# Two graph layers in fp32 on one core: x turned by DVE and moves, masked exponentials in place, new instruction orders

## The chip, the cores and the metric

The kernel runs on one core of a Trainium2 chip. The metric is the device time of one execution in microseconds (us). The core has a matrix engine (TensorE, PE in the profile, with its weight loads as PEld), three engines for elementwise work (VectorE, DVE; ScalarE, ACT; GpSimd, POOL), and an engine that here does nothing but start transfers (SyncE, SP). Each engine runs its own instructions in the order in which they are written, and waits on semaphores for the others.

## What is computed

Eight batches, each with 1024 nodes of 128 channels and a 1024 x 1024 adjacency matrix of zeros and ones, all in fp32. Two layers with a norm each:

```python
u = x @ x.T / sqrt(128)                      # 1024 x 1024 per batch
delta = softmax(u) * adj
att = delta / (sum(delta, axis=2) + 1e-10)
# left: j > i, self: j == i, right: j < i; h_k = x @ W_k.T + b_k
ctx = att_left @ h_left + att_self @ h_self + att_right @ h_right
x1 = norm(x + relu(ln_w * norm(ctx) + ln_b))
d = (sum(adj, axis=-1) + 1e-5) ** -0.5
out = norm(x1 + (d_i * adj * d_j) @ (x1 @ W1) + b1)
```

## The kernel before

A batch is cut into eight blocks i of 128 rows, and into two halves of four blocks (HB = 4). For each block, PE makes the scores u (`scores`, six matmuls of 512 columns, since x is split into a high and a low part in a faster format), DVE takes the row maximum (`row_max`), ACT the exponential (`exps`), DVE multiplies it by the adjacency rows and sums (`masked`), PE turns the product by eight transposes (`turn_d`), ACT copies it out of the accumulator memory (`d_out`), and PE multiplies it with the projected rows (`context_far`, and `context_near` for the diagonal block, for which POOL makes three masked copies in `masks`). Each `project` of a block is followed by `add_bias` on DVE, for the projections share one bank, ps_m.

The second layer needs the adjacency matrix turned. DVE turns it in squares of 32 x 32 (`turn_blocks`, from a_rows to a_blk), and sixteen on-chip transfers for each half (`move_blocks`, issued by SP, L280) put the squares where they belong: in aT, for the last batch in a_rows itself. `gather` multiplies them with the rows of the first layer (x1p), `second_product` with W1 into ps_m, and `add_out` and `stats_f` on DVE follow it. The norms c, x and f each go through DVE (`stats_*`), POOL (`scale_*`), and ACT or POOL.

x itself is also needed turned. Before, PE does that in every batch: `turn_x(b, k)` makes four transposes (L397) for half k into ps_m; ACT's `x_high` (L775) copies them, scaled and rounded, to xT_hi, and DVE's `x_low` (L1027) subtracts to get xT_lo. The exponentials go to e_rows, the masked ones to d_rows, two buffers each: `exps(g)` waits for `masked(g-2)`, and `masked(g)` for `turn_d(g-2)`.

The order of the work on each engine is written out by hand in three functions, `first_batches` (batches 0 and 1), `batch` (2 to 6, in a loop) and `last_batches` (7, the last); b is the batch whose scores are made, p the one before, whose second layer runs beside it. In `batch` PE opens with `turn_x(b, 0)`, `scores(p, 7)`, `turn_d(p, 5)`, `turn_x(b, 1)`. SP takes loads, moves and stores in one order too: a wait on one holds up all behind it.

Of the kernel before, what the change touches and what calls it, by code (L numbers as in the profile page):

```python
# [11 lines left out]
P = 128  # L12
Q = 32
# [12 lines left out]
def two_layer_graph_kernel(nc, x, adj, Wl, bl, Ws, bs, Wr, br, ln_w, ln_b, W1, b1, out):  # L26
# [5 lines left out]
    MOVES = 16 * NQ * NQ  # L32
    SHRINK = float(H) ** -0.25
    assert H == P and NB == 8 and HALF == 512

    with ExitStack() as ctx:  # L36
# [11 lines left out]
        wraw = sb("wraw", [P, 3, H])  # L48
# [10 lines left out]
        xT_lo = sb("xT_lo", [P, 2, N], F32R)  # L59
        h_sum = sb("h_sum", [P, 2, NB, 3 * H])  # L60
# [3 lines left out]
        e_rows = sb("e_rows", [P, 2, N])  # L64
        d_rows = sb("d_rows", [P, 2, N])
# [6 lines left out]
        fin = sb("fin", [P, NB, H])  # L72
        junk = sb("junk", [P, N], mybir.dt.bfloat16)
# [37 lines left out]
        xt_tr = sem("xt_tr")  # L111
        xt_hi = sem("xt_hi")
# [83 lines left out]
        def x_bank(b, k):  # L196
            return ps_y[:, :] if b == 0 and k else ps_m[:, :]
# [54 lines left out]
        def _(sp):  # L252
            def load_x(b):
                wait(sp, xt_tr, 2 * (b - 1))
                wait(sp, x_added, NB * (b - 1))
                sp.dma_start(x_rows[:, b % 2, :, :], x_block_rows(x, b, 0, N)).then_inc(x_in[b % 2], 16)
# [26 lines left out]

            def load_weights():
# [15 lines left out]
            def first_batches(b, p):  # L300
# [5 lines left out]
                next_x(p)  # L306
                load_a(p, 1)
                load_norm_constants()
                load_a(p, 2)
                load_a(p, 3)  # L310
                load_a(p, 4)
                load_a(p, 5)
                next_a(p, 0)
                load_a(p, 6)
                load_a(p, 7)
                next_a(p, 1)
# [4 lines left out]
                next_a(p, 5)  # L321
                move_blocks(p, 1)
                next_a(p, 6)
                next_a(p, 7)
                next_x(b)
                next_a(b, 0)
                store(p, 0, HB)
                next_a(b, 1)
                next_a(b, 2)
                next_a(b, 3)  # L330
                move_blocks(b, 0)
                store(p, HB, NB)
                next_a(b, 4)
                move_blocks(b, 1)
                next_a(b, 5)
                next_a(b, 6)
                next_a(b, 7)

            def batch(b, p):

# [3 lines left out]
                next_a(b, 2)  # L344
                next_a(b, 3)
                store(p, 0, HB)
                move_blocks(b, 0)
                next_a(b, 4)
                store(p, HB, NB)
                next_a(b, 5)  # L350
                next_a(b, 6)
                move_blocks(b, 1)
                next_a(b, 7)

            def last_batches(b, p):

                move_blocks(b, 0)
# [1229 lines left out]
```

## Time and profile before

| | us |
|---|---|
| median of 3 runs (463.78 to 465.43) | 463.79 |
| the profiled execution, its own time | 465.88 |
| its span, first to last instruction | 464.2 |
| PE busy | 449.6 |
| DVE busy | 385.9 |
| ACT busy | 296.0 |
| POOL busy | 296.0 |

The page gives the busy time of each engine over the span; the windows give it for a stretch, the waits say who stood idle for whom, and the timelines list instructions by their start. A row of PE that is merged from several matmuls lasts a little longer than the engine needs for them, since they are pipelined: the distance of two starts is what counts. The granted clock of PE is 0.993 over the span.

### The profile page before, as it was taken

Reading aid. Unit: us, or ns where it says so; the run is one execution under the profiler, and the core shown is the slowest. Engines: PE = TensorE matmul, PEld = TensorE weight load, DVE = VectorE, ACT = ScalarE, POOL = GpSimd, SP = SyncE. Lnnn points to the kernel's source line nnn. Section 1 sums busy time; section 2 is a strip of 40 time slices with the busy share of each in tenths; the row PEclk is TensorE's granted clock in tenths of the full one; section 3 lists DMA queues with packets and bytes.
Section 4 is the critical chain, followed back from the end, with each engine's and each line's share of the span. In section 5 each row is a group of like instructions: output and inputs, shape, how many; then the busy total and the mean of one; then the engine's idle time right before and its main releaser. Section 6 shows DMA issues by size and latency. Waiting matters only on the chain. (4 is left out here: it accounts for less than half of the span.)

```text
span 464.2 us, 8778 instructions
## 1 busy us (share of the span) xinstructions
PE 449.6 (97%) x2711; PEld 364.3 (78%) x2711; DVE 385.9 (83%) x678; ACT 296.0 (64%) x611; POOL 296.0 (64%) x364
## 2 busy tenths in 40 slices
PE   7999999999999999999999999999999999999793
PEld 4799987697967978599776997769886798877562
DVE  3989998898878898788888988789897887998705
ACT  2867787785574876566685765658558676757410
POOL 2324766678655867468663875739665578678762
PEclk9999999999999999999999999999999999999988
DMA  7654739695860897418981289804997066377701
GB/s 174 244 179 114 209 80 241 189 237 141 250 227 1 197 272 208 142 45 195 271 236 73 72 200 270 277 1 108 256 222 234 0 165 200 72 188 172 183 23 45
DMA packets 64269, 76.72 MB, mean 165 GB/s; under 512 B 5696, under 2 KB 56000, under 8 KB 64224
## 3 DMA queue, kind: packets, MB, share of 16 engines
q1 hardware_dynamic: 64160, 76.11, 61.2%
q8 instruction: 22, 0.36, 0.4%
q14 instruction: 23, 0.19, 0.1%
q0 software_dynamic: 64, 0.07, 0.1%
HBM read 38.40 MB, written 4.19 MB: 92 GB/s over the span
## 5 line engine op out<-in xcount | busy, mean ns | idle before, releaser
L783 ACT ACTIVATE e_rows<-ps_u,nmax 128x1024 f32<-128x1024 f32 x62 | 69.0, 1113 | 69.9 <-DVE nmax L1036 69.6
L449 PE MATMUL ps_c<-h_sum,dT 128*128 128x128 f32 x896 | 110.4, 275 | 0.0
L1373 POOL TENSOR_TENSOR dM<-dT,parts 128x384 f32<-128x384 f32 x64 | 68.4, 1068 | 64.9 <-ACT dT L790 55.8
L449 PEld LDWEIGHTS ps_c<-h_sum,dT 128*128 128x128 f32 x896 | 107.0, 192 | 2.5 <-issue 1.4
L469 PE MATMUL ps_y<-aT,x1p 128*128 128x512 f32 x224 | 101.7, 592 | 0.0
L1036 DVE TENSOR_REDUCE nmax<-ps_u 128x1 f32<-128x1024 f32 x62 | 75.5, 1217 | 22.7 <-PE ps_u L376 22.2
L1044 DVE CUSTOM_DVE_ANT_0 d_rows<-e_rows,a_rows 128x1024 f32<-128x1024 f32 x64 | 84.9, 1327 | 7.8 <-PE ps_d L434 7.7
L790 ACT ACTIVATE dT<-ps_d 128x1024 f32<-128x1024 f32 x64 | 65.2, 1018 | 27.7 <-PE ps_d L434 21.3
L1051 DVE STREAM_TRANSPOSE a_blk<-a_rows 128x1024 f32<-128x1024 f32 x64 | 77.9, 1230 | 0.0
L469 PEld LDWEIGHTS ps_y<-aT,x1p 128*128 128x128 f32 x224 | 40.8, 190 | 37.8 <-issue 37.3
L434 PE MATMUL ps_d<-parts,d_rows 128*128 128x128 f32 x512 | 66.8, 273 | 1.4 <-DVE dsum L1044 1.2
L796 ACT ACTIVATE junk<-a_rows 128x1024 bf16<-128x1024 f32 x64 | 67.1, 1048 | 0.7 <-DMA a_rows<-in_adj_dram 0.5
L434 PEld LDWEIGHTS ps_d<-parts,d_rows 128*128 128x128 f32 x512 | 58.3, 141 | 9.7 <-DVE dsum L1044 3.9
L374 PE MATMUL ps_u<-xT_hi 128*128 128x512 f32 x124 | 56.3, 454 | 0.0
L376 PE MATMUL ps_u<-xT_hi,xT_lo 128*128 128x512 f32 x124 | 49.0, 395 | 0.0
L375 PE MATMUL ps_u<-xT_lo,xT_hi 128*128 128x512 f32 x124 | 48.8, 394 | 0.0
L247 DVE TENSOR_TENSOR h_sum<-ps_m,bias_bc 128x384 f32<-128x384 f32 x64 | 35.3, 552 | 8.5 <-PE ps_m L376 6.3
L455 PE MATMUL ps_c<-h_sum,dM 128*128 128x128 f32 x256 | 39.0, 275 | 0.0
L1438 POOL TENSOR_TENSOR power_f<-var_f,minus_half 128x4 f32<-128x4 f32 (+1 forms) x17 | 16.6, 977 | 32.1 <-DVE nmean_f L1130 32.1
L455 PEld LDWEIGHTS ps_c<-h_sum,dM 128*128 128x128 f32 x256 | 34.3, 192 | 1.4 <-issue 1.4
L231 POOL TENSOR_TENSOR c_rows<-c_rows,lnw_bc 128x512 f32<-128x512 f32 x15 | 25.1, 1674 | 13.9 <-ACT c_rows L809 13.9
L1413 POOL TENSOR_TENSOR power_x<-var_x,minus_half 128x4 f32<-128x4 f32 (+1 forms) x17 | 22.5, 1324 | 17.7 <-DVE var_x L1107 17.6
(92 smaller groups left out, 710.7 us busy)
## 6 DMA issues: line engine op xcount, KB each, us to landing
a_rows<-in_adj_dram SPq DMA_DIRECT2D x64, 512.0 KB, 5.2
aT<-a_blk SPq DMA_DIRECT2D x224, 128.0 KB, 2.4
x_rows<-in_x_dram SPq DMA_DIRECT2D x8, 512.0 KB, 5.1
a_rows<-a_blk SPq DMA_DIRECT2D x32, 128.0 KB, 2.4
out_dram<-fin SPq DMA_DIRECT2D x15, 256.0 KB, 2.7
out_dram<-fin SPq DMA_DIRECT2D x2, 128.0 KB, 1.8
wraw<-in_L_gnn_Wl_dram SPq DMA_DIRECT2D x1, 64.0 KB, 3.4
wraw<-in_L_gnn_Wr_dram SPq DMA_DIRECT2D x1, 64.0 KB, 3.1
```

Of the source, the lines that this page charges most:

```text
L374: pe.matmul(o, hi_l, hi_r, start=True, stop=False)
L434: last = pe.transpose(ps_d[:, j, :], d_rows[:, i % 2, j * P:(j + 1) * P], ident)
L449: pe.matmul(ps_c[:, c_place(b, i), :], dT[:, i % 2, j, :], h_sum[:, b % 2, j, k * H:(k + 1) * H], start=t == 0, stop=False)
L455: last = pe.matmul(ps_c[:, c_place(b, i), :], dM[:, i % 2, k, :], h_sum[:, b % 2, i, k * H:(k + 1) * H], start=False, stop=k == 1)
L469: last = pe.matmul(y_bank(b, i0, i1), gathered(b)[:, j, :], turned(b)[:, i0:i1, :, j, :].rearrange("p i q c -> p (i q) c"), start=j == 0, ...
L783: act.activation(e_rows[:, i % 2, :], u_bank(b, i), ACT.Exp, bias=nmax[:, i % 2:i % 2 + 1], accum_out=zsum[:, i:i + 1]).then_inc(exp_done, 1)
L790: act.activation(dT[:, i % 2, :, :], ps_d[:, :, :], ACT.Copy).then_inc(dt_out, 1)
L796: act.activation(junk[:, :], a_rows[:, i, :], ACT.Copy, accum_out=deg[:, i:i + 1])\
L1036: dve.tensor_reduce(nmax[:, i % 2:i % 2 + 1], u_bank(b, i), AX.X, ALU.max, negate=True)\
L1044: dve.tensor_tensor_reduce(out=d_rows[:, i % 2, :], in0=e_rows[:, i % 2, :], in1=a_rows[:, i, :], scale=1.0, scalar=0.0, op0=ALU.mult, op1 ...
L1051: dve.transpose(a_blk[:, i, :, :, :], a_rows[:, i, :].rearrange("p (j m c) -> p m j c", m=NQ, c=Q))\
L1373: pool.tensor_tensor(dM[:, i % 2, :, :], dT[:, i % 2, i, :].rearrange("p (a c) -> p a c", a=1).to_broadcast([P, 3, P]), parts[:, :, :], AL ...
```

## The change

- From batch 2 on, `turn_x` on PE is gone. `turn_rows(b)` on DVE turns the rows of batch b+1 in squares of 32 x 32, `move_rows(b)` on SP puts them into x_turned by sixteen transfers, and `x_high` and `x_low` read from there; `x_low` takes two instructions of 256 elements for each half in place of one of 512 and has both inputs in SBUF.
- The exponentials are written to d_rows, a ring of three, and masked there in place. `exps(g)` now waits for `turn_d(g-3)`, and `masked` no longer waits for PE. e_rows is gone.
- wraw lies in fin. Two of the four first matmuls are shortened from 512 to 384 columns.
- All engines have new orders. `scores(b, 7)`, `turn_d(b, 5)`, `turn_d(b, 6)`, `context_far(b, 4)` and `(b, 5)` and `context_near(b, 4)` are now in batch b's own part; the moves of half 1 go to the start of the next part on SP. In `first_batches` DVE turns the first adjacency block ahead of the first row maximum. In `last_batches` PE makes the last contexts ahead of most of the previous batch's gathers of half 1.

```diff
@@ helpers
+        def x_columns(b, k):
+            if b < 2:
+                return (ps_y if b == 0 and k else ps_m)[:, :]
+            return x_turned[:, NQ // 2 * k:NQ // 2 * (k + 1), :, :]
...
+        def x_pieces(v, b):
+            return [v] if b < 2 else [v[:, q, :, :] for q in range(NQ // 2)]
@@ sync
+            def move_rows(b):
+                sp.wait_ge(rows_turned, b)
+                if b > 1:
+                    sp.wait_ge(xt_split, 2 * (b + 1))
+                for q in range(NQ):
+                    for m in range(NQ):
+                        sp.dma_start(x_turned[m * Q:(m + 1) * Q, q, :, :], x_blk[q * Q:(q + 1) * Q, m, :, :])\
+                          .then_inc(rows_moved, 16)
...
+            def batch(b, p):
+
+                move_blocks(p, 1)
+                next_a(p, 7)
+                next_x(b)
+                next_a(b, 0)
+                next_a(b, 1)
+                move_rows(b)
+                next_a(b, 2)
+                move_blocks(b, 0)
                 next_a(b, 3)
                 store(p, 0, HB)
-                move_blocks(b, 0)
                 next_a(b, 4)
+                next_a(b, 5)
                 store(p, HB, NB)
-                next_a(b, 5)
                 next_a(b, 6)
-                move_blocks(b, 1)
-                next_a(b, 7)
@@ tensor, batch: its start and its end
+                scores(b, 0)
+                m_read_o(p - 1, HB, NB)
+                project(b, 0)
+                context_near(p, 5)
+                turn_d(p, 7)
...
                 second_product(p, HB, NB)
-                context_far(b, 3)
-                context_near(b, 3)
+                context_far(b, 4)
+                turn_d(b, 6)
+                context_near(b, 4)
+                context_far(b, 5)
@@ tensor, last_batches: from the last scores to the first gather of half 1
                 scores(b, 7)
+                context_far(b, 4)
                 m_read_h(b, 7)
                 second_product(p, 0, HB)
+                context_near(b, 4)
+                turn_d(b, 6)
                 gather(p, HB, NB, 0, 1)
                 context_far(b, 5)
                 gather(p, HB, NB, 1, 2)
+                turn_d(b, 7)
                 context_near(b, 5)
                 context_far(b, 6)
                 context_near(b, 6)
                 context_far(b, 7)
                 context_near(b, 7)
+                gather(p, HB, NB, 2, 4)
+                gather(p, HB, NB, 4, 6)
+                gather(p, HB, NB, 6, 8)
+                m_read_o(p, 0, HB)
+                second_product(p, HB, NB)
+                gather(b, 0, HB, 0, 4)
+                gather(b, HB, NB - 2, 0, 2)
@@ scalar
             def exps(b, i):
                 g = NB * b + i
                 act.wait_ge(nmax_ready, g + 1)
-                wait(act, d_ready, g - 1)
+                wait(act, dt_tr, g - 2)
@@ vector
-                wait(dve, dt_tr, g - 1)
-                dve.tensor_tensor_reduce(out=d_rows[:, i % 2, :], in0=e_rows[:, i % 2, :],
+                dve.tensor_tensor_reduce(out=d_rows[:, g % 3, :], in0=d_rows[:, g % 3, :],
...
+            def turn_rows(b):
+                dve.wait_ge(x_in[(b + 1) % 2], 16 * ((b + 1) // 2 + 1))
+                wait(dve, rows_moved, ROW_MOVES * (b - 1))
+                dve.transpose(x_blk[:, :, :, :],
+                              x_rows[:, (b + 1) % 2, :, :].rearrange("p i (m c) -> p m i c", m=NQ, c=Q))\
+                   .then_inc(rows_turned, 1)
@@ vector, first_batches
                 add_bias(p, 0)
+                turn_blocks(p, 0)
                 row_max(p, 0)
@@ vector, batch: its start, the place of turn_rows, its end
+                x_low(b, 0)
+                x_low(b, 1)
+                masked(p, 7)
+                turn_blocks(p, 7)
...
+                stats_x(p, HB, NB)
+                turn_blocks(b, 1)
                 masked(b, 3)
+                turn_blocks(b, 2)
+                row_max(b, 5)
                 row_sums(b, 0)
                 turn_blocks(b, 3)
+                turn_rows(b)
                 masked(b, 4)
...
+                row_max(b, 7)
+                add_self(b, 0, HB)
+                stats_c(b, 0, HB)
                 masked(b, 6)
                 add_out(p, HB, NB)
                 stats_f(p, HB, NB)
@@ vector, last_batches: between the last row maximum and the last turned block
+                row_max(b, 7)
+                add_out(p, 0, HB)
+                stats_f(p, 0, HB)
+                masked(b, 7)
                 turn_blocks(b, 4)
                 turn_blocks(b, 5)
+                stats_x(b, 0, HB)
                 turn_blocks(b, 6)
                 turn_blocks(b, 7)
```

## Rows read from the trace of the kernel before

**Rows 1.** The page: busy us, share of the span, instructions of each engine.

```profile
PE 449.6 (97%) x2711; PEld 364.3 (78%) x2711; DVE 385.9 (83%) x678; ACT 296.0 (64%) x611; POOL 296.0 (64%) x364
```

**Rows 2.** Windows: one batch; busy us (instructions) by engine, PEclk, DMA share, GB/s.

```profile
172.08:227.66 55.58, 55.15 (x337) 44.79 (x337) 47.94 (x83) 36.54 (x78) 36.59 (x44) 1.00 0.63 169
```

**Rows 3.** Waits of PE, 5 to 440 us: waiter, releaser, total us, times, longest.

```profile
PE ps_d L434 <- DVE dsum L1044: 1.2, 3, 0.4
```

**Rows 4.** Timeline, start of the last batch: start us, us, engine, line, operation, count.

```profile
371.10 0.60 PE L397 MATMUL ps_m<-parts,x_rows 128*128 128x128 f32 x4
371.54 1.04 PE L434 MATMUL ps_d<-parts,d_rows 128*128 128x128 f32 x8
```

**Rows 5.** Two lines of DVE by tile and line: duration ns min/median/max, first and last start.

```profile
L1027 DVE SCALAR_TENSOR_TENSOR xT_lo<-ps_m,xT_hi x15: 653/686/692, 6.8 to 372.4; 128x512 fp32r<-128x512 f32 x15
...
L1102 DVE SCALAR_TENSOR_TENSOR c_rows<-c_rows,x_rows x17: 426/1418/1486, 52.0 to 440.4; 128x512 f32<-128x512 f32 x15, 128x256 f32<-128x256 f32 x2
```

**Rows 6.** Timeline of POOL and DVE in one stretch.

```profile
225.52 0.99 POOL L1373 TENSOR_TENSOR dM<-dT,parts 128x384 f32<-128x384 f32 x1
225.67 1.92 DVE L1044 CUSTOM_DVE_ANT_0 d_rows<-e_rows,a_rows 128x1024 f32<-128x1024 f32 x1
...
227.99 1.21 DVE L1044 CUSTOM_DVE_ANT_0 d_rows<-e_rows,a_rows 128x1024 f32<-128x1024 f32 x1
```

**Rows 7.** Lines L280 and L256 (SP): durations ns, and issue to landing.

```profile
L280 SPq DMA_DIRECT2D aT<-a_blk x224: 591/606/1902, 41.3 to 410.5; - x112
...
DMA to landing us min/median/max: 2.3/2.4/6.8
...
DMA to landing us min/median/max: 3.8/5.1/8.5
```

**Rows 8.** Timeline of SP: one group of sixteen moves.

```profile
261.93 12.41 SPq L280 DMA_DIRECT2D aT<-a_blk  x16
```

**Rows 9.** The start: PE, DVE, and the landing of the first adjacency block.

```profile
13.33 0.41 PE L374 MATMUL ps_u<-xT_hi 128*128 128x512 f32 x1
...
10.67 1.21 DVE L1036 TENSOR_REDUCE nmax<-ps_u 128x1 f32<-128x1024 f32 x1
...
L263 SPq DMA_DIRECT2D a_rows<-in_adj_dram x1: 432/432/432, 4.3 to 4.3; - x1
...
DMA to landing us min/median/max: 7.3/7.3/7.3
```

**Rows 10.** Timeline of PE from the last scores to the last batch's gathers.

```profile
417.04 1.05 PE L481 MATMUL ps_m<-w_sb,yT 128*128 128x128 f32 x8
...
419.49 1.02 PE L469 MATMUL ps_y<-aT,x1p 128*128 128x512 f32 x2
420.35 0.61 PE L455 MATMUL ps_c<-h_sum,dM 128*128 128x128 f32 x4
420.80 1.73 PE L449 MATMUL ps_c<-h_sum,dT 128*128 128x128 f32 x14
422.36 1.04 PE L434 MATMUL ps_d<-parts,d_rows 128*128 128x128 f32 x8
...
440.54 3.95 PE L469 MATMUL ps_u<-a_rows,h_sum 128*128 128x256 f32 x10 [2.85 <-DMA a_rows<-a_blk]
```

**Rows 11.** What precedes the last moves: DVE, ACT, and SP (410 to 442 us).

```profile
423.81 2.36 DVE L1051 STREAM_TRANSPOSE a_blk<-a_rows 128x1024 f32<-128x1024 f32 x2
...
425.58 1.06 ACT L796 ACTIVATE junk<-a_rows 128x1024 bf16<-128x1024 f32 x1
...
L280 SPq DMA_DIRECT2D a_rows<-a_blk x32: 585/602/2141, 414.7 to 438.0; - x32
```

**Rows 12.** Windows: the stretch after PE's last long wait, columns as in rows 2.

```profile
440.00:444.00 4.00, 3.46 (x9) 2.83 (x10) 1.41 (x5) 1.59 (x4) 2.95 (x6) 0.57 0.23 66
```

**Rows 13.** Timeline of DVE: add_out and the end of stats_f.

```profile
452.88 1.13 DVE L1118 SCALAR_TENSOR_TENSOR fin<-ps_m,dinv,x1b 128x128 f32<-128x128 f32 x4 [11.18 <-PE ps_m L481]
...
454.99 0.16 DVE L1130 TENSOR_SCALAR nmean_f<-stats_f 128x4 f32<-128x4 f32 x1
```

More of the change, by code:

```diff
@@ L305, in first_batches @@
                 load_a(p, 0)
-                next_x(p)
                 load_a(p, 1)
@@ new lines, in first_batches @@
+                turn_d(p, 7)
+                m_read_h(b, 2)
+                project(b, 3)
+                scores(b, 2)
+                context_near(p, 6)
+                m_read_h(b, 3)
+                project(b, 4)
+                context_far(p, 7)
+                m_read_h(b, 4)
+                project(b, 5)
+                context_near(p, 7)
+                scores(b, 3)
+                turn_d(b, 0)
+                gather(p, 0, HB, 0, 1)
+                m_read_h(b, 5)
+                project(b, 6)
@@ new lines, in first_batches @@
+                gather(p, 0, HB, 1, 3)
+                scores(b, 4)
+                m_read_h(b, 6)
+                project(b, 7)
+                gather(p, 0, HB, 3, 4)
+                turn_d(b, 1)
+                context_far(b, 0)
+                context_near(b, 0)
+                context_far(b, 1)
+                turn_d(b, 2)
+                scores(b, 5)
+                context_near(b, 1)
+                turn_d(b, 3)
+                context_far(b, 2)
+                turn_d(b, 4)
@@ new lines, in first_batches @@
+                context_near(b, 2)
+                context_far(b, 3)
+                gather(p, 0, HB, 4, 8)
+                scores(b, 6)
+                gather(p, HB, NB, 0, 1)
+                context_near(b, 3)
+                gather(p, HB, NB, 1, 2)
+                m_read_h(b, 7)
+                second_product(p, 0, HB)
+                gather(p, HB, NB, 2, 4)
+                gather(p, HB, NB, 4, 7)
+                scores(b, 7)
+                gather(p, HB, NB, 7, 8)
+                turn_d(b, 5)
@@ new lines, in first_batches, with batch @@
+                m_read_o(p, 0, HB)
[4 more added lines that the diff above has]
+                turn_d(b, 6)
+            def batch(b, p):
+                scores(b, 0)
+                m_read_o(p - 1, HB, NB)
+                project(b, 0)
+                context_near(p, 5)
+                turn_d(p, 7)
+                m_read_h(b, 0)
+                project(b, 1)
+                context_far(p, 6)
```

827 lines of the change are left out of this document (371 added, 456 removed).

## The prediction

> **What bounds the kernel now.** I read the page first, then windows of one batch, then the waits of the engine they point to. PE is busy for 449.6 of 464.2 us, DVE for 83% of it [rows 1]. The share alone could mislead, for a merged row of PE covers its pipeline's latency too, so the window of one batch decides: PE busy for 55.15 of 55.58 us, at a granted clock of 1.00, which is 2.4 GHz [rows 2]. The waits say the same from the other side: between 5 and 440 us the costliest wait of PE, turn_d for the masked rows, comes to 1.2 us in three places [rows 3]. So between the start and the end the time is the sum of PE's own work, and an edit gains what it takes off PE, unless it makes PE wait. Outside that stretch there are two losses: the start (PE waits for the first data and biases) and the end, where PE stands idle 2.85 us for the last on-chip moves [rows 10] and then runs at a granted clock of 0.57 in the mean of 4 us [rows 12], between the two levels of 2.4 and 1.2 GHz: (1 - 0.57) x 4 = 1.7 us more.
>
> **The change part by part, in PE's time.**
>
> Removed: turn_x of batches 2 to 7, twelve times four transposes. What four cost is the distance of two starts, 371.54 - 371.10 = 0.44 us [rows 4] (the 0.60 us of the row itself has the pipeline's latency in it). 12 x 0.44 = 5.3 us. This is certain as work, since no other instruction of PE takes its place, and it is the whole gain that the trace supports directly. The two shortened first matmuls run before the first data can be used; I cost that at nothing, for the first add_bias waits for the bias loads anyway.
>
> Added on DVE: turn_rows, six transposes of 128 x 1024. Two of the kind take 2.36 us [rows 11], so 1.2 each, 7 us in all. x_low: before, two instructions of 0.686 us a batch [rows 5]. After, four of 256 elements, both inputs in SBUF. The nearest row is stats_x's addition in L1102, whose 256-wide form is the minimum of 426 ns [rows 5]; back to back they overlap a little, so 1.5 to 1.7 us. The other bound is the same line's 512-wide form in its usual state, 1418 ns: four half-wide ones then come to 2 x 1.42 = 2.84 us. DVE rises from 385.9 to about 395 us, which it has room for; what matters is where. x_low stands at the border of two batches, and scores(b, 0) is now the first thing that PE wants of the new one. After the previous second_product PE has left: context_far(4), turn_d(6), context_near(4), context_far(5). By distances of starts a context_far is 422.36 - 420.80 = 1.56, a context_near 420.80 - 420.35 = 0.45 [rows 10], a turn_d eight transposes, 0.88 [rows 4]: 4.45 us. In that time DVE must do add_out and stats_f, which take 454.99 + 0.16 - 452.88 = 2.27 us [rows 13], and x_low, 1.5 to 1.7: 3.8 to 4.0, and some 0.2 for hand-overs. That just fits; I take 0 to 0.3 us of PE idle a border, six borders.
>
> What may stretch x_low is in the trace. masked took 1.92 us while POOL's masks ran beside it and 1.21 without [rows 6]; L1102, which has the same kind of inputs, is nearly always in the long state. x_low from PSUM never is: 653 to 692 ns over all its uses [rows 5]. The Trainium skill (GPSIMD Engine Reference, 1. Specifications) says that POOL contends for SBUF with DVE instructions that have two SBUF inputs. By that rule the new x_low is exposed and the old was not, which speaks against this part; the trace agrees on masked and on L1102. By order of the lists POOL has scale_f and then affine near the border, and affine waits for ACT's norm_c, which stands behind x_high; so I take the short state and keep the long one as a rival.
>
> Added on SP: sixteen moves a batch. An aT move of 128 KB takes 0.606 us to issue [rows 7], and a group of sixteen 12.4 us [rows 8]; these are a quarter of the size, so at most that. SP then has three groups a batch, at most 37 us, and some ten loads and stores, in a batch of 55: it fits. The chain in time, counted from scores(b, 0): stats_x(p, HB) lets go of the x rows at about 25 us, the load lands 5.1 us later (8.5 at worst) [rows 7], at 30 to 33; turn_rows stands behind seven DVE steps and is done at about 34; the moves are out at 46 and landed at 48 to 49 (2.4 us [rows 7]); x_high wants them at about 50. Margin 1 to 2 us, more if the smaller moves issue faster. Queued behind the group are next_a(b, 2) and move_blocks(b, 0); the first needs no more than to land before the next batch's third masked, the second is wanted only at the next batch's first gather, some 14 us into it. Both come in time.
>
> In place and in a ring of three: same instruction, same size. L1102 writes over its own input too, and its 256-wide 426 ns [rows 5] are in line with masked's 1.21 us for 1024 elements out of place [rows 6], so in place costs nothing that a row shows. exps(g) now waits for turn_d(g-3), which in the new orders is always three steps earlier, and masked loses its wait for PE. Price 0 on both, and the cover is PE's saturation.
>
> The orders, in the middle: with all steps at their rows' durations, the hand-over that is nearest to late is exps(3) before scores(4), within 0.2 us. Now PE idles 55.58 - 55.15 = 0.43 us a batch; I expect 0.3, for a gain of 0.8 us over six or seven batches. Bounds: -2.5 (all idle gone) to +4.
>
> The start: turn_blocks(p, 0) now stands ahead of row_max(p, 0), which began at 10.67; it needs the adjacency block that was issued at 4.3 and landed 7.3 us later, at 11.6, and takes 1.2: row_max begins at 12.8, 2.1 us later. exps(0) is as much later, and PE's scores(2), which began at 13.33 [rows 9], waits for it. Some of it is had back, since idle times that stood behind it are filled: +1.0 us, bounds 0 and +2.1.
>
> The end, counted from the end of scores(7), 417.04 [rows 10]. Before: DVE is done turning at 423.81 + 2.36 = 426.17, ACT with the degrees at 426.64, the last of the moves starts at 438.0 [rows 11], PE goes on at 440.54, 13.5 us after the start of the sixteen moves at about 427.0. After, DVE does: row_max 1.2, wait for second_product (PE: context_far 1.56, eight matmuls 0.9) until 2.6, add_out and stats_f 2.3, masked 1.3, two turns 2.4, stats_x 2.1, two turns 2.4: 13.1. With 13.5 for the moves: 26.6. PE gets there after four context_far (6.2), four context_near (1.8), two turn_d (1.8), two second_product (1.8), and gathers of eight steps at 420.35 - 419.49 = 0.86 (6.9) and of the first four of the last batch (3.4): 21.9. So the wait is 4.7 us, not 2.85, and the slow clock behind it stays at 1.7. One of the two waits for yT at the very end is filled by a gather, -0.7. Sum of the end: +1.9 - 0.7, rounded down to +0.9, since a wait of ACT or POOL may as well shrink. This is the second unsure term: bounds -5 (moves in time, clock kept) and +3.
>
> Sum: -5.3 - 0.8 + 1.0 + 0.9 = -4.2 us on the profiled 465.88, whose span is 464.2; the same difference on the median of the runs, which lies 2.1 below the profiled execution: 463.79 - 4.2 = 459.6.
>
> **The rivals.**
> A, x_low in the long state, or DVE late at the border. The long x_low is 1.2 us more than the short one, of which 0.2 is margin: 1.0 a border, six borders: 459.6 + 6 = 465.6; if every second one is hit, 462.6. For it: the long state of L1102. Against: what stands on POOL there. The trace of after shows it as PE idle before scores(b, 0).
> B, slower: SP. The rows of x come late since SP is one queue: the x load waits for stats_x(p, HB, NB), and the moves behind it for turn_rows. The x load at its worst landing (3.4 us later than the median) and moves at the full cadence put x_high 2 to 4 us behind, and PE has nothing before scores(b, 0) that could run: each us over the margin costs one at six borders. It outweighs the gain from 0.7 us a border on; with 2 us it gives 459.6 + 12 = 471.6.
> C, the last moves are in time. PE's wait and the slow clock are gone: 459.6 - 4.7 - 1.7 = 453.2. For it: PE has 2 us more work ahead of the wait than before. Against: DVE turns the last blocks some 4 us later.
> That the change doesn't do what it says is no rival: the transposes are gone by the text.
>
> **How the numbers follow.** My case 0.64 (its own range 456.5 to 461.5), A 0.18, B 0.08, C 0.10. The range reaches down into C and up into A: 455 to 465. A measurement of this kernel can tell 0.5%, 2.3 us, from no change: faster is below 461.5, slower above 466.1. Faster: 0.62 of my case, 0.10 of C, 0.03 of A: 0.75. Slower: 0.08 of B and 0.02 of A: 0.10. Same: 0.15.
>
> **What would show it.** L397 on PE sixteen times, in place of 64, and the windows' PE work lower by 0.88 us a batch; PE's busy share in a batch of the middle still above 99%, the batch 54.6 to 54.9 us long. x_low's instructions at 0.43 us (my case) or 0.7 (A). PE's wait for xT_lo or xT_hi at the borders under 0.3 us (else A or B; B if x_high waits for the moves). The last wait for the moves at 4 to 5 us (else C). Wrong would be above all a PE that waits in the middle of batches for nmax, exponentials or h_sum, which I costed at 0.3 us a batch.

## The result and the profile after

The changed kernel takes 463.38 us in the median of 20 runs (461.15 to 465.00), the kernel before 464.73 us of 20 (463.49 to 466.19). The ratio of the means is 0.9964, 95% interval 0.9951 to 0.9977: 1.7 us less (1.35 by the medians), where 4.2 us less was forecast. It is faster, then, but by less than the 0.5% that the forecast took as the least to tell from no change, and it lies 1.9 us above the 461.5 below which it would have been called faster. The range of 455 to 465 us holds the time. In the runs further below, one execution, of the kernel with all edits and two queues, took 925.38 us, about twice the others, and is left out of every median, ratio and product.

The page's row for PE (busy us, share of the span, instructions), which answers to [rows 1]; the span of this execution is 461.6 us, its time 463.36 us:

```profile
PE 444.2 (96%) x2663; PEld 357.7 (77%) x2663; DVE 388.8 (84%) x696; ACT 296.8 (64%) x611; POOL 310.9 (67%) x364
```

PE lost 5.4 us of busy time and 48 instructions, yet the span fell by 2.6 us only: PE's idle time rose from 464.2 - 449.6 = 14.6 to 461.6 - 444.2 = 17.4 us. To find where, I cut both executions into the same three stretches (columns as in [rows 2]). Before:

```profile
0.00:60.00 60.00, 56.76 (x362) 49.32 (x363) 48.83 (x76) 38.68 (x76) 23.73 (x33) 1.00 0.61 178
60.00:360.00 300.00, 298.91 (x1805) 241.04 (x1804) 260.06 (x444) 202.68 (x422) 200.61 (x236) 1.00 0.67 180
360.00:464.20 104.20, 93.92 (x548) 73.95 (x546) 76.98 (x161) 54.65 (x114) 71.61 (x96) 0.97 0.47 117
```

After, and below it one batch of the middle, from scores(b, 0) to the next scores(b, 0):

```profile
0.00:60.00 60.00, 53.34 (x338) 45.20 (x339) 46.90 (x70) 39.09 (x77) 23.66 (x34) 1.00 0.61 195
60.00:360.00 300.00, 299.67 (x1800) 241.14 (x1799) 267.98 (x468) 203.81 (x422) 213.31 (x238) 1.00 0.67 182
360.00:461.60 101.60, 91.23 (x529) 71.41 (x527) 73.90 (x160) 53.88 (x115) 73.90 (x94) 0.97 0.52 133
...
176.34:230.64 54.30, 54.23 (x329) 43.91 (x329) 48.10 (x86) 36.84 (x77) 39.46 (x45) 1.00 0.69 184
```

Idle is the length less PE's busy time. In the first 60 us it went from 3.24 to 6.66: 3.4 us more, at a granted clock of 1.00 in both. In the middle it went from 1.09 to 0.33, 0.8 less, and at the end from 10.28 to 10.37. So the middle gave what was forecast, the end cost 0.1, and the start idled 3.4 more where I had written 1.0. The batch of 54.30 us stands against the 55.58 of [rows 2].

Not all of the 3.4 is lost time. These are the first matmuls and the first projection, before and then after:

```profile
1.51 3.78 PE L392 MATMUL ps_u<-d_rows 128*128 128x512 f32 x4 [1.51 <-DVE d_rows L1016]
...
8.12 0.41 PE L374 MATMUL ps_m<-wT_hi,xT_hi 128*128 128x384 f32 x1 [0.85 <-DVE wT_lo L1020]
...
1.51 3.35 PE L421 MATMUL ps_u<-d_rows 128*128 128x512 f32 x4 [1.51 <-DVE d_rows L1038]
...
7.52 0.41 PE L403 MATMUL ps_m<-wT_hi,xT_hi 128*128 128x384 f32 x1 [1.26 <-DVE wT_lo L1042]
```

The shortened first matmuls give PE 0.4 us less to do and the wait for the low weights is 0.4 longer, yet the first projection starts 0.6 us sooner. So 0.4 us only passed from busy to idle: some 3.0 us are lost in the start, and 5.0 of the 5.4 us of busy time are other work.

The waits of PE between 5 and 440 us show the same (waiter, releaser, total us, times, longest); in [rows 3] the costliest of before was 1.2:

```profile
PE ps_m L403 <- DVE h_sum L263: 3.7, 4, 1.4
PE ps_m L403 <- DVE wT_lo L1042: 1.3, 1, 1.3
PE ps_c L478 <- issue: 0.9, 1, 0.9
PE ps_m L510 <- issue: 0.8, 1, 0.8
```

All four waits for h_sum (add_bias, L263) lie before 52 us: 0.88 at 10.60, 1.40 at 14.18, 0.80 at 23.88 and 0.65 at 51.20 us; the same line took 0.5 in all before. The first is no loss: before, PE went on at 10.81 there, and the two other profiled executions of the changed kernel have three such waits, 2.9 in sum. The other three, 2.85 us, are nearly the whole 3.0. The timeline of DVE for the one at 14.18 (start us, us, line, tiles), with PE's row below it:

```profile
11.31 1.25 DVE L1074 STREAM_TRANSPOSE a_blk<-a_rows 128x1024 f32<-128x1024 f32 x1 [0.77 <-DMA a_rows<-in_adj_dram]
12.47 1.19 DVE L1060 TENSOR_REDUCE nmax<-ps_u 128x1 f32<-128x1024 f32 x1
13.58 0.54 DVE L263 TENSOR_TENSOR h_sum<-ps_m,bias_bc 128x384 f32<-128x384 f32 x1
...
14.18 0.44 PE L403 MATMUL ps_m<-wT_hi,xT_hi 128*128 128x384 f32 x1 [1.40 <-DVE h_sum L263]
```

turn_blocks(p, 0) waits 0.77 us for the adjacency block and takes 1.25. The row maximum stands behind it, and behind that the bias of step 1, without which project(2) has no PSUM to write to. So the moved transpose is paid by PE not through the exponentials, as I had reasoned, but through add_bias.

The waits at 23.88 and 51.20 have another origin. There PE's new list has two projections with nothing between them (the earlier ones start at 22.31 and 49.86; in the old list a scores, a turn_d or a context stands between), and the second must wait until add_bias, 0.55 us, has emptied ps_m. DVE's row and PE's at the later place:

```profile
50.58 0.56 DVE L263 TENSOR_TENSOR h_sum<-ps_m,bias_bc 128x384 f32<-128x384 f32 x1 [0.21 <-PE ps_m L405]
...
51.20 0.45 PE L403 MATMUL ps_m<-wT_hi,xT_hi 128*128 128x384 f32 x1 [0.65 <-DVE h_sum L263]
```

DVE had itself stood idle 0.21 us for PE, so nothing in DVE's list was in the way. At 23.88 masked was, until 23.28, for about 0.3 us of that wait.

**One quantity used below.** Executions of one and the same kernel differ by 2 to 4 us, and nearly all of it is the mean granted clock: the 20 of the changed kernel stand in groups near 0.989, 0.993 and 0.996, and span times clock has a standard deviation of only 0.4 us around 458.4 (457.5 to 459.3). I call that product the span at full clock. It is 461.0 and 460.7 for the kernel before in two sets, and 458.7 and 458.8 for the changed one beside it. It strips the clock from a comparison; the runs' ratio keeps it, and is the time that counts. With few executions its scatter is 0.4 to 1.0 us, so differences of 0.7 are near what it can tell.

The profiled executions show where the groups come from. In two of the changed kernel's three, the stretches from 440 to 448 us have a lowered clock (0.71 and 0.86 in one, 0.63 and 0.94 in another); the third, with the same wait of 2.2 us before them, has none:

```profile
440.00:444.00 4.00, 3.11 (x11) 2.20 (x12) 1.63 (x8) 1.76 (x4) 2.89 (x8) 1.00 0.16 46
444.00:448.00 4.00, 3.65 (x16) 2.07 (x15) 0.00 (x0) 0.60 (x1) 3.62 (x8) 1.00 0.03 8
```

Their means are 0.993, 0.993 and 0.996. Other executions lose about as much in the first 60 us (0.66 from 8 to 12 us in the run with the turned block later, mean 0.992), and one with a lowered clock near both ends (0.57 from 8 to 12 us and 0.83 from 430 to 440, in the kernel with all edits and two queues) has 0.989. Such a stretch is worth about 1.7 us, (0.29 + 0.14) x 4 in the first, and whether it comes differs between executions of one kernel.

### The profile page after: what moved, and what is told of

It reads as the page before. It is cut to its first block and busy times, and to the rows that moved or that the text cites. A ratio compares the mean times of both kernels' runs of the same rounds, so it can differ in the third digit from the quotient of the medians.

```text
span 461.6 us, 8799 instructions
## 1 busy us (share of the span) xinstructions
PE 444.2 (96%) x2663; PEld 357.7 (77%) x2663; DVE 388.8 (84%) x696; ACT 296.8 (64%) x611; POOL 310.9 (67%) x364
## 5 line engine op out<-in xcount | busy, mean ns | idle before, releaser
L498 PE MATMUL ps_y<-aT,x1p 128*128 128x512 f32 x224 | 104.3, 592 | 0.0
L805 ACT ACTIVATE d_rows<-ps_u,nmax 128x1024 f32<-128x1024 f32 x62 | 68.9, 1112 | 50.3 <-DVE nmax L1060 50.2
L1067 DVE CUSTOM_DVE_ANT_0 d_rows<-d_rows,a_rows 128x1024 f32<-128x1024 f32 x64 | 84.8, 1326 | 0.4 <-ACT d_rows L805 0.4
L498 PEld LDWEIGHTS ps_y<-aT,x1p 128*128 128x128 f32 x224 | 39.7, 190 | 29.9 <-issue 29.4
L263 DVE TENSOR_TENSOR h_sum<-ps_m,bias_bc 128x384 f32<-128x384 f32 x64 | 35.3, 551 | 14.7 <-PE ps_m L405 12.4
L484 PEld LDWEIGHTS ps_c<-h_sum,dM 128*128 128x128 f32 x256 | 36.0, 191 | 4.5 <-issue 2.9
L255 POOL TENSOR_SCALAR fin<-fin,power_f,shift_f 128x128 f32<-128x128 f32 x56 | 36.2, 659 | 0.3
L1421 POOL TENSOR_TENSOR power_c<-var_c,minus_half 128x4 f32<-128x4 f32 (+1 forms) x17 | 22.2, 1304 | 20.1 <-DVE nmean_c L1119 20.1
L403 PE MATMUL ps_m<-wT_hi,xT_hi 128*128 128x384 f32 x64 | 28.4, 444 | 5.0 <-DVE h_sum L263 3.7
```

The lines of the kernel that those rows point to most:

```text
L403: pe.matmul(o, hi_l, hi_r, start=True, stop=False)
L484: last = pe.matmul(ps_c[:, c_place(b, i), :], dM[:, i % 2, k, :], h_sum[:, b % 2, i, k * H:(k + 1) * H], start=False, stop=k == 1)
L498: last = pe.matmul(y_bank(b, i0, i1), gathered(b)[:, j, :], turned(b)[:, i0:i1, :, j, :].rearrange("p i q c -> p (i q) c"), start=j == 0, ...
L805: act.activation(d_rows[:, g % 3, :], u_bank(b, i), ACT.Exp, bias=nmax[:, i % 2:i % 2 + 1], accum_out=zsum[:, i:i + 1]).then_inc(exp_done, 1)
L1067: dve.tensor_tensor_reduce(out=d_rows[:, g % 3, :], in0=d_rows[:, g % 3, :], in1=a_rows[:, i, :], scale=1.0, scalar=0.0, op0=ALU.mult, op1 ...
```

## The experiments

The theory: PE's sum is the time; the removed transposes came off it whole, and what is missing went into waits of PE at the start, by the orders of DVE's and PE's lists, with small ones at the end. Rivals: the work removed isn't worth its pitch, the new path of x costs something in the middle, or the missing time is the wait for the last moves. Each kernel below is an edit of the changed one, and ratios are to the kernel before. The changed kernel itself ran as a mark in two of the sets.

**The changed kernel again.**

> The changed kernel once more, on the chip of the runs beside it, as their mark. Theory: 1.3 to 2.5 us faster than the kernel before; the mean granted clock of its executions is about 0.0015 lower than that of the kernel before (0.7 us of a span), because it has more idle time of PE at the start and at the end, behind which the clock is granted late. Rival (the clock is the chip's, not the kernel's): the mean clocks agree within 0.0005.

Measured 462.95 us, ratio 0.9954 (0.9931 to 0.9977). The mean clocks are 0.9944 for the kernel before and 0.9939 for this one, the 0.0005 of the rival and not the 0.0015 of the theory.

> The changed kernel once more, beside the others of this set: 0.995 to 0.998 of the kernel before, span times clock 458.4 to 458.8.

Measured 462.55 us, ratio 0.9960 (0.9943 to 0.9977). Full-clock spans as above.

**Is PE the sum?** 48 transposes that nothing reads, written to ps_y behind the second product of six batches:

```
+    def idle_turns():
+        for j in range(8):
+            pe.transpose(ps_y[:, j % 4 * P:(j % 4 + 1) * P], ident, ident)
...
     second_product(p, HB, NB)
+    idle_turns()
```

> The changed kernel with eight more transposes on PE in each of batches 1 to 6, after the second product of half 1, that turn the identity into a free bank and that nobody reads: 48, as many as the change took away. Theory (PE is the sum): the gain of the transposes is given back in full, 5.3 us slower than the changed kernel, ratio to the kernel before 1.007 to 1.009, each batch of the middle 0.88 us longer than 54.3. Rival (PE has slack in the changed kernel, and DVE or the exponentials set its pace): under 2 us slower.

Measured 470.35 us, ratio 1.0106 (1.0076 to 1.0137); full-clock span 464.4, which is 5.7 to 6.0 above the changed kernel. The work added is 48 x 0.11 = 5.3 us by the pitch of [rows 4]. In time it is 6.9 us above the changed kernel, more than the 1.007 to 1.009 expected, since its mean clock is 0.9915. The middle of its profiled execution is as full as that of the changed kernel, so nothing absorbed it:

```profile
60.00:360.00 300.00, 299.67 (x1821) 242.87 (x1821) 262.56 (x458) 200.31 (x414) 210.67 (x233) 1.00 0.67 182
```

So 48 transposes are worth their pitch in either direction, and the term of -5.3 us stands. The few tenths above it are, in part, a last wait for the moves that is longer by 0.7 us in that execution; that part isn't settled.

**The turned block ahead of the first row maximum.**

```
     add_bias(p, 0)
-    turn_blocks(p, 0)
     row_max(p, 0)
...
     add_bias(p, 7)
+    turn_blocks(p, 0)
     turn_blocks(p, 1)
     row_max(p, 5)
```

SP also asks for batch 1's first adjacency block two loads later; that was not tried apart.

> The changed kernel, but at the start DVE turns the first adjacency block only just ahead of the second one, and SP asks for batch 1's first block two loads later; all else is as changed. Theory (start): the changed kernel loses its gain in the first 60 us, where PE idles 3.4 us more than in the kernel before, 1.8 us of that since the first row maximum starts at 12.47 instead of 10.67 us. Then this run is 1.5 to 2 us faster than the changed kernel, ratio to the kernel before 0.992 to 0.993, and the idle time before the third projection (1.4 us) goes. Rival (idle time moves on): the first exponentials then meet other waits, and the run is within 0.5 us of the changed kernel, ratio 0.996.

Measured 460.96 us, ratio 0.9908 (0.9886 to 0.9930), full-clock span 457.2 in four executions: 1.2 to 1.5 us under the changed kernel of the other sets (458.4 to 458.7), a little less than expected. The wait at 14.18 is gone, one of 0.7 for the exponentials came, the two behind it (23.88 and 51.20) stayed. So this line costs what the term of +1.0 had been written for, and the rest of the 3.0 stays.

**The whole old start.** First only the lists up to the fifth row maximum; DVE's edit, with PE's, ACT's and SP's lists taken back likewise:

```
     add_bias(p, 0)
-    turn_blocks(p, 0)
     row_max(p, 0)
     add_bias(p, 1)
     row_max(p, 1)
-    masked(p, 0)
-    row_max(p, 2)
     add_bias(p, 2)
-    row_max(p, 3)
+    masked(p, 0)
     add_bias(p, 3)
-    masked(p, 1)
+    row_max(p, 2)
...
+    row_max(p, 4)
+    masked(p, 3)
+    turn_blocks(p, 0)
     turn_blocks(p, 1)
```

> The changed kernel with the old order of scores, projections, row maxima and masked steps up to the fifth row maximum, on PE, DVE, ACT and SP. Theory (start): the whole loss of the first 30 us comes back, 2.5 to 3 us against the changed kernel, ratio to the kernel before 0.989 to 0.991; turn_x of batch 1 starts some 2.7 us earlier than in the changed kernel. Rival (only the turned block matters): the same as the run with the block turned later, within 0.4 us. Second rival: the time is given back before 60 us, where add_bias and the row maxima are late.

Measured 463.53 us, ratio 0.9960 (0.9939 to 0.9981), full-clock span 458.1. My graft made a wait of its own: scores(5) stood at once behind turn_d(2) and waited 2.0 us for the exponentials. So this run said little of the 2.5 to 3 us expected, and I grafted the order up to scores(6), with DVE's and ACT's steps beside it (PE's edit, against the first graft):

```
     turn_d(p, 2)
-    scores(p, 5)
     m_read_h(p, 7)
     turn_x(b, 0)
     context_far(p, 0)
     context_near(p, 0)
+    scores(p, 5)
     context_far(p, 1)
```

> As the run with the old start, but with the old order carried on to the sixth scores: these stand behind turn_x of batch 1 and the first contexts again, so that PE has work while ACT makes the fifth exponentials. Theory (the loss is in the order of the start, and the 2.2 us wait at 26 us of the run before was made by the graft): PE's idle time in the first 60 us falls from 9.2 to 6 or 7 us, 2.3 to 3 us faster than the changed kernel in the same call. Rival (the idle time moves on to the steps that follow, whose order expects the new start): within 1 us of the changed kernel.

Measured 461.88 us, ratio 0.9911 (0.9888 to 0.9935), full-clock span 457.0. The window and the waits from 5 to 60 us:

```profile
0.00:60.00 60.00, 54.76 (x346) 47.20 (x347) 48.34 (x72) 40.77 (x79) 26.11 (x35) 1.00 0.65 197
...
PE ps_m L403 <- DVE wT_lo L1042: 1.3, 1, 1.3
PE ps_u L403 <- ACT d_rows L805: 1.1, 1, 1.1
PE ps_m L403 <- DVE h_sum L263: 1.0, 2, 0.7
```

PE is busy 1.42 us more than in the changed kernel, which agrees with 1.7 less at full clock. The h_sum waits fell from 3.7 to 1.0. The gain expected, 2.3 to 3, is missed. PE's busy time is still 2.0 short of before: 0.4 is the shortened first matmuls and no loss, 1.1 is a wait for exponentials that the graft places late, and 0.5 is more h_sum, since 0.65 at 49.6 us remains in the second batch, whose order I left alone.

**The new path of x with the old orders.** The moves of x go into SP's old list ahead of move_blocks(b, 0), turn_rows behind turn_blocks(b, 3), and the lists of PE, DVE and ACT stay those of before but for what the path itself adds and removes. On SP, against the changed kernel:

```
-    move_blocks(p, 1)
-    next_a(p, 7)
-    next_x(b)
     next_a(b, 0)
+    next_x(b)
     next_a(b, 1)
-    move_rows(b)
     next_a(b, 2)
-    move_blocks(b, 0)
     next_a(b, 3)
+    move_rows(b)
     store(p, 0, HB)
+    move_blocks(b, 0)
...
     next_a(b, 6)
+    move_blocks(b, 1)
+    next_a(b, 7)
```

> The changed kernel's x path and ring of three, but all lists of steps as in the kernel before, less turn_x from batch 2 on and with turn_rows and move_rows put in after the turn of block 3. Theory (PE is the sum, the orders are not what gains): 4.5 to 5.5 us faster than the kernel before, ratio 0.988 to 0.990, faster than the changed kernel, since the start is the old one. Rival (the new orders are needed, for with the old ones PE waits at the border for x_low or for row maxima): 0 to 2.5 us faster than before, with waits of PE of 0.5 to 1 us a batch.

Measured 470.35 us, ratio 1.0110 (1.0089 to 1.0131), full-clock span 462.4. DVE, SP, ACT and PE at the border of the second and third batch:

```profile
85.60 1.25 DVE L1085 STREAM_TRANSPOSE x_blk<-x_rows 128x1024 f32<-128x1024 f32 x1 [0.29 <-DMA x_rows<-in_x_dram]
...
88.83 1.73 SPq L280 DMA_DIRECT2D a_rows<-in_adj_dram  x3
90.62 10.08 SPq L308 DMA_DIRECT2D x_turned<-x_blk  x16
100.81 11.17 SPq L297 DMA_DIRECT2D aT<-a_blk  x16
...
102.02 0.63 ACT L801 ACTIVATE xT_hi<-x_turned 128x512 fp32r<-128x512 f32 x1 [9.74 <-DMA x_turned<-x_blk]
...
103.70 1.09 PE L463 MATMUL ps_d<-parts,d_rows 128*128 128x128 f32 x4 [7.79 <-ACT dT L816]
```

The x rows are turned at 86.85, but SP, behind three loads in its list, starts the sixteen moves at 90.62 and needs 10.08 us for them. ACT stands still 9.7 us for the first, with d_out queued behind it, and PE 7.8 us. That is rival B's mechanism, once. At four later borders PE waits 0.23 to 0.24 us for x_low, and a batch takes 54.8 us. The run is 5.1 us slower than the kernel before, outside both the theory (4.5 to 5.5 faster) and its rival (0 to 2.5 faster). At full clock it is 1.3 slower; the rest is clock, 0.987 in the mean against 0.995, with 0.66 from 104 to 108 us, behind the wait. So the new orders are no ornament of the change: they pull the moves of x out of the way and bring 0.5 us a batch (54.3). Other places for the moves in the old list weren't tried.

**The end: the added bias ahead of masked.** PE's idle 0.92 us at 396.99 (context_far(0), which reads h_sum) has these rows of POOL and DVE in front of it:

```profile
393.23 2.09 POOL L1464 TENSOR_TENSOR x1b<-x1b,b_bc 128x512 f32<-128x512 f32 x1
...
392.14 2.02 DVE L1067 CUSTOM_DVE_ANT_0 d_rows<-d_rows,a_rows 128x1024 f32<-128x1024 f32 x1
...
394.10 2.31 DVE L1067 CUSTOM_DVE_ANT_0 d_rows<-d_rows,a_rows 128x1024 f32<-128x1024 f32 x1
...
396.34 0.55 DVE L263 TENSOR_TENSOR h_sum<-ps_m,bias_bc 128x384 f32<-128x384 f32 x1
```

Two masked take 2.02 and 2.31 us beside POOL's additions of 128 x 512, and 1.2 at the start without them. The edit:

```
     masked(b, 2)
-    masked(b, 3)
     add_bias(b, 7)
+    masked(b, 3)
```

> One edit on the changed kernel: in the last batch the added bias of step 7 stands ahead of masked of step 3. Theory (the 1.06 us that PE idles at 397 before the first far product is the wait for that bias behind a stretched masked): the wait is gone or under 0.3 us, masked of step 3 and what hangs on it come some 0.8 us later without PE waiting for it, span times clock lower by 0.8 to 1.1 us. Rival (the time comes back as a longer wait for the last moves, which stand behind DVE's list): wait at 440 longer by as much, sum unchanged.

Measured 462.16 us, ratio 0.9955 (0.9932 to 0.9978); full-clock span 457.5, 1.25 below the mark of its set. PE doesn't wait there any more, and DVE's second masked, now behind the bias, starts 0.5 us later against the first and takes 1.83. The runs' ratio, though, is that of the mark, since its executions had a mean clock of 0.993 where the mark had 0.995. Its wait for the last moves is 2.1 us, as before the edit, so the rival (it comes back there) falls; in time, the 1 us can't be told from nothing by these runs.

**The end: the last two turned blocks first.**

```
     turn_blocks(b, 5)
-    stats_x(b, 0, HB)
     turn_blocks(b, 6)
     turn_blocks(b, 7)
+    stats_x(b, 0, HB)
```

> One edit on the changed kernel: the last two turned blocks stand ahead of the sum of x (2.1 us) in the last batch. Theory (the last wait for the moves is the time by which DVE hands over the last turned block): the sixteen moves start some 2 us earlier and the wait of 2.3 us before the last gathers goes to under 0.5 us; the half of the output that needs the sum of x comes 2 us later and the wait of PE for it, 0.9 us, grows by up to 2 us, so the sum is 0 to 1.5 us lower. Rival (PE's order gives it all back): no change in span times clock.

Measured 461.18 us, ratio 0.9928 (0.9903 to 0.9952), full-clock span 458.1, 0.7 below the mark, which its scatter (456.6 to 458.8 in six executions) doesn't tell from nothing. PE's wait for the moves (2.2 us in the changed kernel) is gone from the list, and 0.7 for the sum of x came:

```profile
PE ps_m L510 <- issue: 1.1, 2, 0.8
...
PE ps_y L498 <- ACT h_sum L831: 0.7, 1, 0.7
```

In time it brings 1.4 us, twice what it brings at full clock: its six executions have a mean clock of 0.997 (0.995 to 0.998), the mark's twelve 0.995 (0.992 to 0.997).

**The end: half of the last moves on ACT.**

```
+    def move_rest(b):
+        act.wait_ge(a_turned, NB * (b + 1))
...
+        for q in range(NQ // 2, NQ):
+            for m in range(NQ):
+                act.dma_start(turned(b)[m * Q:(m + 1) * Q, blocks_of(1), q, :, :],
+                              a_blk[q * Q:(q + 1) * Q, blocks_of(1), m, :, :])\
+                   .then_inc(a_moved[1], 16)
...
     diagonal(b, 7)
+    move_rest(b)
     norm_x(b, 0, HB)
```

SP keeps the eight with q below NQ // 2.

> The changed kernel, but of the last sixteen moves (last batch, half 1) ACT issues eight, between diagonal(7) and norm_x. Theory (SP's issue of 0.65 us a move sets the end of PE's wait at 440.6): the moves are all out 5 us earlier, the wait of 2.4 us and the slow clock behind it (1.7 us in the profiled run) go, 2.4 to 4 us faster than the changed kernel, if norm_x stays in time on ACT. Rival (something else arrives no earlier: the rows of the first layer, at 441 to 443 us): the wait is replaced by one for x1p, under 1 us faster.

Measured 464.15 us, ratio 0.9971 (0.9955 to 0.9988), full-clock span 459.4, 0.7 above the mark, where 2.4 to 4 faster was expected. The timeline of ACT and PE:

```profile
428.47 6.30 ACTq L841 DMA_DIRECT2D a_rows<-a_blk  x8
434.88 1.65 ACT L831 ACTIVATE h_sum<-c_rows,shift_x,scale_x 128x128 f32<-128x128 f32 x4 [6.96 <-issue]
436.43 0.57 ACT L860 ACTIVATE yT<-ps_y 128x512 f32<-128x512 f32 x1
...
437.10 2.04 PE L510 MATMUL ps_m<-w_sb,yT 128*128 128x128 f32 x8 [3.36 <-issue]
```

The wait for the moves is gone, but ACT spends 6.30 us on issuing eight of them, y_out stands behind, and PE waits 3.36 us for yT, where it had waited 0.78. A queue on an engine that does other work isn't a free queue.

**Together.** The edits above in one kernel: the old start (the second graft), the bias ahead of masked, the two turned blocks first, and the two queues:

> The changed kernel with the whole old start, the last sixteen moves by two queues, the last two turned blocks ahead of stats_x at the end, and, in the last batch, add_bias(7) ahead of masked(3), for which context_far(0) waited 1.06 us while two masked steps took 2.0 and 2.3 us beside POOL. Theory: the sum of the parts, 2.5 + 3 + 1 = 5 to 7 us faster than the changed kernel, 7 to 9 us faster than the kernel before, ratio 0.981 to 0.985. Rival: the parts at the end overlap, and the sum is 3 to 4 us.

Measured 459.87 us in the median of five, ratio 0.9869 (0.9844 to 0.9893), full-clock span 455.5: some 3 us under the changed kernel, the rival's 3 to 4 and not the 5 to 7 of the theory, which had counted 3 for the two edits of the end. The same without the last of these, all moves on SP:

> The old start, the added bias of step 7 ahead of masked of step 3, and the last two turned blocks ahead of the sum of x in the last batch; the moves all on SP. Theory (starting order and the two small waits cost what they idle, splitting the moves between queues gives nothing): span times granted clock 455.5 or below, some 1.5 us below the old start alone, and time not above that of the same kernel with two queues (460.1), 1.7 to 3 us below the changed kernel. Rival (the two queues were worth something after all, since the wait for the moves went): 1 to 2.4 us above it, with a wait for the moves of at least 2.3 us before the last gathers.

Measured 458.39 us (457.98 to 458.54), ratio 0.9863 (0.9838 to 0.9887), full-clock span 455.3, mean clock 0.997. This is the fastest kernel of the study, 4.2 us below the changed kernel in the same set. At full clock it is 3.4 below, and the three edits apart gave 1.7, 1.25 and 0.7, so they nearly add up. PE's waits from 380 us on:

```profile
PE ps_m L510 <- issue: 1.1, 2, 0.8
PE ps_y L498 <- ACT h_sum L831: 0.6, 1, 0.6
...
PE ps_u L498 <- DMA a_rows<-a_blk: 0.2, 1, 0.2
```

With two queues the wait for yT is 2.0 us, here 0.8, at a full-clock span that is the same within its scatter. The second queue buys nothing once the blocks are turned early.

## Why the prediction was right and where it was wrong

**The removed transposes: right.** PE's busy time fell by 5.4 us against 5.3 (that it fits so closely is chance, for 0.4 of it is the shortened first matmuls), and 48 transposes put back as idle ones cost at least as much.

**The middle: right, rivals A and B both absent.** x_low by tile and duration (min/median/max), all borders, with POOL's row beside one of them:

```profile
L1050 DVE SCALAR_TENSOR_TENSOR xT_lo<-x_turned,xT_hi x24: 412/416/419, 99.4 to 372.0; 128x256 fp32r<-128x256 f32 x24
...
208.26 1.12 POOL L1470 TENSOR_TENSOR power_f<-var_f,minus_half 128x4 f32<-128x4 f32 x1 [1.19 <-DVE nmean_f L1160]
...
208.09 1.42 DVE L1050 SCALAR_TENSOR_TENSOR xT_lo<-x_turned,xT_hi 128x256 fp32r<-128x256 f32 x4
```

All 24 are short, four take 1.42 us, and the border idles 0.2 by the distance of starts (no wait of PE is listed there). What POOL does beside them has 4 elements a partition. So the price came from the right row (426 ns in [rows 5]), and the condition that I had attached, what stands on POOL there, was the right one to ask. The Trainium skill (GPSIMD Engine Reference, 1. Specifications) has POOL contend with DVE instructions that have two SBUF inputs: the masked of the last batch agree, with 2.02 and 2.31 us beside POOL's large additions; x_low beside a tiny POOL instruction isn't longer than its nearest row. I had looked for the rule at x_low, and it took its toll at another two-input instruction that the new order put beside POOL's.

The sixteen x moves took 10 us (a median of 591 ns each) in place of the bound of 12.4, and were never late in the new order. A batch is 54.30 us, a little under the 54.6 to 54.9 that I named. DVE's busy time rose by 2.9 us and not by the 9 that I had: the sum of x (L1132 now, L1102 before) takes 681 ns in the median against 1418 [rows 5], which I had not looked for.

**The start: the step that failed.** The term was +1.0, with bounds of 0 and +2.1; PE idles 3.4 us more there, of which 3.0 are lost. Two steps of it failed. I followed one chain only, turned block, row maximum, exponentials, scores(2), and gave back a part of its 2.1 us because other idle times would be filled. What I left out is who else stands behind on DVE: add_bias(p, 1), which PE needs earlier than the exponentials. Even so the size was about right: taking back the turned block alone returns 1.2 to 1.5 us.

The larger miss is that I costed only this one edit of the start and put every other new order there at nothing, without a reason. PE's own new list has two projections back to back at 23.88 and at 51.20 us, and waits 0.80 and 0.65 for add_bias there: 1.45 us, most of the 2.0 by which the term was short. No run took back these two places alone. The old start returned 1.7 us in all, with a wait of 1.1 of its own and the 0.65 of the second batch still in it.

**The end: its sum was closer than its parts.** I said a wait of 4.7 us for the moves, with a slow clock of 1.7 behind it, and +0.9 in all. Measured at the profiled execution:

```profile
415.29 1.72 PE L478 MATMUL ps_c<-h_sum,dT 128*128 128x128 f32 x14
...
425.35 2.36 DVE L1074 STREAM_TRANSPOSE a_blk<-a_rows 128x1024 f32<-128x1024 f32 x2
...
440.59 1.13 PE L498 MATMUL ps_u<-a_rows,h_sum 128*128 128x256 f32 x4 [2.24 <-DMA a_rows<-a_blk]
...
440.00:444.00 4.00, 3.41 (x10) 2.44 (x11) 1.42 (x7) 1.75 (x4) 3.02 (x7) 0.71 0.08 23
444.00:448.00 4.00, 4.00 (x10) 1.78 (x8) 0.00 (x0) 0.21 (x1) 3.62 (x8) 0.86 0.11 32
```

Counted from the end of scores(7), at 415.29, DVE is done turning after 12.4 us, where I had 13.1, and PE goes on 12.9 us later, where I had 13.5. PE itself is there after 23.1 us (440.59 - 2.24 - 415.29), where I had 21.9, mostly since it had waited 0.78 at 433.78, which was not in my sum. So the wait is 4.7 - 0.7 - 0.6 - 1.2 = 2.2 us, shorter than I had it but not gone, as rival C would have it. The wait of 0.92 at 396.99 lies ahead of this count and doesn't shorten it; with the 0.78 it is what the end lost where I hadn't looked, and idle time merely changed its place: +0.1 in place of +0.9. That the sum came so near is luck. The clock term was as said, (0.29 + 0.14) x 4 = 1.7 us, but the third profiled execution of this kernel had no such stretch behind the same wait.

**From the profile to the runs.** By the two profiled executions the gain is 2.5 us in time, and in span -5.4 + 3.4 - 0.8 + 0.1 = -2.7, which is the 2.6 shown above but for rounding. The runs show 1.7, and in the two other sets 2.1 and 1.9. The full-clock spans of the two sets with marks differ by 2.3 and 1.9, so some of it is that the two profiled executions weren't at the same point of their scatter; the mean clocks of before and changed (0.994 to 0.994, 0.995 to 0.995) differ by less than 0.001, 0.2 us. The rest of the forecast's error is the start. The forecast time of 459.6 had 0.9 against it besides, since the 463.79 it was taken from was the median of three runs and that of 20 is 464.73. That the range holds 463.38 is owed to its width: it reached above 461.5 for rival A, which did not occur.

## What to carry to other kernels

When an instruction is put ahead of others on an in-order engine, list every instruction behind it and who needs each first; the victim here was not the next one but the one after it. In the list of the busy engine, look for two steps that share a buffer with nothing between them. Cost the start and the end of a pipelined kernel edit by edit, as the saturated middle: in the middle the new orders were worth 0.5 us a batch, in the first 25 us one line was worth 1.2 to 1.5 us. Compare also when the same work starts, not idle time alone: 0.4 us of the idle time here was work that had been taken out. And once PE is full, compare orders by span at equal clock, then by time.

## What the runs showed of the hardware that I had not expected

- The granted clock is part of a kernel's time even with nothing else changed: 0.989 to 0.997 over 20 executions of one kernel, some 2 us up or down. The two kernels without the 2 us wait for the last moves, and all moves on SP, had means of 0.997, against 0.993 to 0.995 for the changed one, and none of their eleven executions was below 0.995. That a filled wait keeps the clock fits this, but eleven are few, and the changed kernel too kept it in some executions in spite of the wait.
- Moves of 32 KB take nearly as long to issue as moves of 128 KB: sixteen in 10.08 us on SP against 11.17 us in the rows above. On ACT eight moves of 128 KB took 6.30 us, 0.79 each against 0.6 to 0.7 on SP.
- Masked and POOL's large additions don't share, they take turns. The stretch at 392 us (DVE's rows stand above), on POOL:

```profile
392.05 1.04 POOL L1461 TENSOR_TENSOR x1b<-c_rows,power_x 128x512 f32<-128x512 f32 x1
...
395.29 2.25 POOL L247 TENSOR_TENSOR c_rows<-c_rows,lnw_bc 128x512 f32<-128x512 f32 x1
```

  POOL's L1461 ends at 393.09. The masked that started at 392.14 ends at 394.16, 1.07 behind it. POOL's L1464 started at 393.23 and ends at 395.32, 1.16 behind that masked; the next masked ends at 396.41, 1.09 behind L1464; and L247 at 397.54, 1.13 behind that. Each takes about its undisturbed time (1.2 for masked) from the end of the other's. A pair on [rows 6] does the same: POOL's ends at 226.51 and masked at 227.59. The Trainium skill (SBUF — State Buffer, SBUF: two separate sides) says that whichever of the two starts first holds the shared ports for its whole instruction; all five of these ends agree. So the price of such a meeting can be written down ahead: the later one is longer by what is left of the earlier one. In [rows 6] I had read a state, 1.92 against 1.21, where the rows held the rule.

  It doesn't hold for every POOL instruction that starts first. POOL's power of 4 elements a partition takes about 1.0 us, and x_low and masked that start within it are not longer. L1470 above runs to 209.38 and the four x_low beside it still take 1.42 us; and here masked takes its 1.21:

```profile
225.09 1.01 POOL L1421 TENSOR_TENSOR power_c<-var_c,minus_half 128x4 f32<-128x4 f32 x1 [3.15 <-DVE nmean_c L1119]
...
225.40 1.21 DVE L1067 CUSTOM_DVE_ANT_0 d_rows<-d_rows,a_rows 128x1024 f32<-128x1024 f32 x1
```

  So against such small instructions that rule of the Trainium skill isn't borne out here, and the measurement decides.
